# Expert attention with heads in 32-row tiles of TensorE, unpadded keys, and maxima taken over causal query blocks two units ahead

## The reference, cut to what matters

```
sx = einsum('bsh,ndh->bnsd', x, hl_w) + hl_b          # x is 32 x 188 x 64 after a layernorm
q = einsum('bnsd,neod->bneso', sx, wq)                # 4 heads n, 4 experts e, d = 16
k = einsum('bnsd,nod->bnso', sx, wk);  v = einsum('bnsd,nod->bnso', sx, wv)
scores = einsum('bnesd,bntd->bnest', q, k) * d**0.5 + causal
att = softmax(scores);  qkv = einsum('bnest,bntd->bnesd', att, v)   # 0 where sx == 0
gs = softmax(gate logits over experts); mixed = sum over e of qkv * gs
# then two layernorms over d, a small gated feed-forward, and the sum with x
```

## Time and profile before

| what | value |
|---|---|
| median of 3 runs | 1999.27 us (1997.89 to 2005.81) |
| profiled execution, its own time | 2006.71 us |
| its span in the trace | 2004.9 us |
| busy in the span: PE, PEld, DVE | 1719.6, 1344.4, 1488.5 us |
| busy in the span: ACT, POOL | 756.6, 690.5 us |
| mean granted TensorE clock | 0.865 |
| first and last record of `ex_R` | 572.9 and 1327.9 us |

### The profile page before, as it was taken

How to read it: one execution, slowest core, us unless ns; L and a number is a source line. 1 busy time by engine, 2 the same in 40 slices (tenths; PEclk the granted TensorE clock), 3 DMA queues, 4 the chain that set the end, 5 groups by cost and what they waited for, 6 DMA issues and landing times. The chain is left out here.

```text
span 2004.9 us, 45616 instructions
## 1 busy us (share of the span) xinstructions
PE 1719.6 (86%) x15064; PEld 1344.4 (67%) x15064; DVE 1488.5 (74%) x4423; ACT 756.6 (38%) x2274; POOL 690.5 (34%) x957
## 2 busy tenths in 40 slices
PE   1499999999769999999999999973999999788887
PEld 1266666666557777777777777752888888677776
DVE  6166676666627898888889888875766665688887
ACT  2245454545324444344344444321222222343442
POOL 2622222222134555545545445532211111322221
PEclk9999999999869999999999999985555555788788
DMA  2000000000000000000000000000000000000000
GB/s 114 1 2 0 0 0 0 0 0 0 1 1 1 1 2 0 0 0 0 0 0 0 0 0 0 1 1 0 1 0 0 0 0 1 1 5 8 4 6 11
DMA packets 6980, 8.13 MB, mean 4 GB/s; under 512 B 6272, under 2 KB 6272, under 8 KB 6784
## 3 DMA queue, kind: packets, MB, share of 16 engines
q1 hardware_dynamic: 6912, 7.25, 1.1%
HBM read 5.71 MB, written 1.54 MB: 4 GB/s over the span
## 5 line engine op out<-in xcount | busy, mean ns | idle before, releaser
L1142 ACT ACTIVATE ex_pT<-ex_T 128x376 f32<-128x376 f32 (+1 forms) x384 | 162.8, 440 | 217.1 <-PE ex_T L1044 207.9
L604 ACT ACTIVATE al_prob<-al_S,al_negmax 94x94 f32<-94x94 f32 (+1 forms) x512 | 146.2, 375 | 180.0 <-DVE al_negmax L731 180.0
L1207 DVE TENSOR_REDUCE ex_negmax<-ex_R 94x2 bf16<-94x376 f32 (+1 forms) x384 | 186.8, 543 | 30.6 <-PE ex_R L1015 30.0
L1044 PE MATMUL ex_T<-ex_qm,ex_kpad 128*128 128x188 f32 x1024 | 189.7, 329 | 0.0
L505 PE MATMUL al_S<-al_kpad,al_qT 128*94 128x376 f32 x384 | 166.5, 516 | 0.0
L1044 PEld LDWEIGHTS ex_T<-ex_qm,ex_kpad 128*128 128x128 f32 x1024 | 163.0, 192 | 5.1
L944 POOL TENSOR_SCALAR_AFFINE_SELECT ex_pT<-ex_pT 128x512 f32<-128x512 f32 x128 | 84.3, 659 | 236.5 <-ACT ex_pT L1142 236.5
L682 POOL TENSOR_TENSOR al_kpad<-al_kT,al_quad_mask 128x1504 f32<-128x1504 f32 x32 | 86.2, 2692 | 186.3 <-ACTq L619 186.3
L731 DVE TENSOR_REDUCE al_negmax<-al_S 94x2 f32<-94x376 f32 (+1 forms) x192 | 99.1, 542 | 62.6 <-PE al_S L506 56.7
L1554 POOL TENSOR_TENSOR ta_kk<-ta_ext 94x320 f32<-94x320 f32 x64 | 60.4, 961 | 246.4 <-DVE ta_qkn L1734 163.0
L1027 PE MATMUL ex_R<-ex_sxT,wsb 128*128 128x188 f32 x256 | 72.3, 364 | 47.5 <-DVE ex_negmax L1207 47.5
(11 more groups left out here) (308 smaller groups left out, 4300.8 us busy)
## 6 DMA issues: line engine op xcount, KB each, us to landing
tok_xin<-x_t SPq DMA_DIRECT2D x4, 760.0 KB, 6.9
wsb<-weights SPq DMA_DIRECT2D x1, 2531.0 KB, 14.2
out<-stream SPq DMA_DIRECT2D x16, 94.0 KB
tok_par<-tok_w SPq DMA_DIRECT2D x1, 4.5 KB, 1.7
```

The costliest lines, as they stand in the source:

```text
L604: last = nc.scalar.activation(p[:, k, cols], S[0:P, k, cols], ACT.Exp, bias=negmax[g % 2][:, m:m + 1])
L1044: last = nc.tensor.matmul(T[:, k, (j % 2) * N:(j % 2 + 1) * N], kpad[par][:, j, 0:K0], qm[e % 2][:], start=True, stop=True)
L1142: nc.scalar.activation(pT[e % 2][rows, k, cols], T[rows, k, cols], ACT.Exp)\
L1207: red(dst, src, AX.X, ALU.max, negate=True).then_inc(sem["r_used"], 1)
```

## The change: what it does

- **Heads in row tiles.** A head's 32 rows of keys and queries are used directly, as a 32-row tile of the array (`tile_position=(32 * n, ...)`). `kpad`, `kpadb`, `quad_mask` and GpSimd's two products a row are gone; ScalarE writes the keys twice instead, in fp32 and bf16.
- **Maxima over three causal blocks.** Queries are split in blocks of 64, 64 and 60, which meet 64, 128 and 188 keys. Two heads lie on the two halves of the partitions, two pairs in two banks of `R`: 12 matmuls of 32 rows x 64 columns, then 4 mask matmuls of 128 rows. VectorE's three reductions read 128, 256 and 376 elements.
- **queries** now writes to the free end of a bank of `T`, with six small matmuls instead of two.
- **scores** is split in heads 0 and 1 and heads 2 and 3, each head in its own bank of `T`; keys 64 to 191 (zero from 188 on) replace keys 128 to 187 in the second product. ScalarE's three exponents become two of 496 elements.
- **Order.** `max_scores` runs two units ahead, at the end of a unit before `weigh`. The order is: scores of heads 0 and 1, queries of the next unit, a fill, scores of heads 2 and 3, a fill, `max_scores`, `weigh`, a fill. The fills q01 and fc1 change places. VectorE's order is unchanged.
- More constants are set up by GpSimd ahead of the stage (29 instructions, from 21).

```diff
+    BLOCKS = [(0, QB, QB), (QB, 2 * QB, QB), (3 * QB, N, K1)]      # first column, keys, queries
+    PAIR = N + K1                                                  # QB = 64, QCOL = 256
-        kpad = two("kpad", [128, NH, N])
-        kpadb = two("kpadb", [128, NH, N], BF16)
+        kT = two("kT", [128, NP])
+        kTb = two("kTb", [128, N], BF16)
-        R = psum("R", [128, 3, 512])
-        T = psum("T", [128, 3, 512])
+        R = psum("R", [128, 2, 512])
+        T = psum("T", [128, NH, 512])
...
+                need(pe, sem["r_used"], 3 * u)
+                for k, (first, keys, _) in enumerate(BLOCKS):
+                    for n in range(NH):
+                        rows, side = slice(32 * n, 32 * n + 32), QB * (n % 2)
+                        nc.tensor.matmul(R[side:side + QB, n // 2, first:first + keys],
+                                         qTb[par][rows, e, QB * k:QB * (k + 1)], kTb[par][rows, 0:keys],
+                                         start=(k == 0), stop=False, tile_position=(32 * n, side), skip_group_check=True)
+                for b in range(2):
+                    two_blocks = R[:, b, 0:4 * QB].rearrange("p (a c) -> p a c", c=2 * QB)[:, :, 0:QB]
+                    nc.tensor.matmul(two_blocks, eye[:], block_mask[:].unsqueeze(1).broadcast_to([128, 2, QB]),
+                                     start=False, stop=True, skip_group_check=True)
+                    last = nc.tensor.matmul(R[:, b, 5 * QB:5 * QB + K1], eye[:], block_mask[:, 0:K1], start=False,
+                                            stop=True, skip_group_check=True)
+                last.then_inc(sem["r_full"], 1)
...
+                nc.tensor.matmul(T[:, 0, QCOL:QCOL + N], w("ewq")[:, e * 128:(e + 1) * 128], sxT[par][:, 0:N],
+                                 start=True, stop=False, skip_group_check=True)
+                for k, (_, _, cols) in enumerate(BLOCKS):
+                    for c in range(2):
+                        last = nc.tensor.matmul(T[:, 0, QCOL + QB * k:QCOL + QB * k + cols],
+                                                negmax[e % 2][:, k, 32 - 32 * c:160 - 32 * c], eye[:, QB * c:QB * c + cols],
+                                                start=False, stop=True, skip_group_check=True)
...
+                for s in range(2):
+                    for n in heads:
+                        rows = slice(32 * n, 32 * n + 32)
+                        if s == 0:
+                            last = nc.tensor.matmul(T[:, n, 0:N], kT[par][rows, 0:K0], qm[e % 2][rows, :], start=True,
+                                                    stop=True, tile_position=(32 * n, 0), skip_group_check=True)
                         else:
+                            last = nc.tensor.matmul(T[:, n, N:PAIR], kT[par][rows, QB:NP], qm[e % 2][rows, K0:N],
+                                                    start=True, stop=True, tile_position=(32 * n, 0),
+                                                    skip_group_check=True)
...
                     nr, ne, npar = (ru, e + 1, par) if e < 3 else (rf, 0, odd)
+                    fr, fe, fpar = (ru, e + 2, par) if e < 2 else (rf, e - 2, odd)
+                    last = None
+                    if valid(ru):
+                        last = scores(ru, par, e, (0, 1))
                     if valid(nr):
-                        max_scores(nr, npar, ne)
-                    if valid(ru):
-                        scores(ru, par, e)
+                        last = queries(nr, npar, ne)
+                    if last is not None:
+                        last.then_inc(sem["tA_full"], 1)
...
-                    if valid(nr):
-                        queries(nr, npar, ne)
+                    if valid(ru):
+                        scores(ru, par, e, (2, 3)).then_inc(sem["tB_full"], 1)
...
+                    if valid(fr):
+                        max_scores(fr, fpar, fe)
                     if e == 0 and valid(rt):
                         weigh(rt, odd, 3)
...
-                for k in range(3):
-                    dve.wait_ge(sem["r_full"], 3 * u + k + 1)
+                dve.wait_ge(sem["r_full"], u + 1)
+                for k, (first, keys, _) in enumerate(BLOCKS):
+                    red(negmax[e % 2][:, k, 48:113:64], R[:, :, first:first + keys], AX.X, ALU.max, negate=True)\
+                        .then_inc(sem["r_used"], 1)
```

More of the change, by code:

```diff
@@ L870, in expert_attention @@
         LN, FRONT, UNIT, TAIL, NORM, MLP, FIN, LAST = range(8)
[L873 to L876, removed]
+        FILLS = [("xT", FRONT), ("znT", MLP), ("sx", FRONT), ("k", FRONT), ("q01", FRONT), ("pickA", TAIL),
+                 ("fg", LAST), ("fc1", MLP), ("pickB", TAIL), ("q23", FRONT), ("v", FRONT), ("fc2", MLP)]
+        PER_ROW = {"sx": 2, "v": 2, "k": 2}
         def valid2(r):
@@ L940, in body @@
                         p = pT[e % 2]
-                        pool.wait_ge(sem["t_used"], 3 * (r * NE + e) + 3)
+                        pool.wait_ge(sem["tB_used"], r * NE + e + 1)
                         pool.sem_inc(sem["settled"], 1)
[L943 to L957, removed]
+                        for first, cols, shift in ((0, K0, 0), (N, K1, QB)):
+                            view = p[:, :, first:first + cols]
+                            nc.gpsimd.affine_select(out=view, in_=view, compare_op=ALU.is_ge, fill=0.0, base=shift,
+                                                    pattern=[[0, NH], [1, cols]], channel_multiplier=-1)\
+                                .then_inc(sem["causal_done"], 1)
                     r = t - LN
@@ L1036, in scores @@
+                return last
+            def scores(r, par, e, heads):
                 u = r * NE + e
                 if e == 0:
[L1038 removed]
+                    pe.wait_ge(sem["k_used"], 2 * (r + 1))
                 pe.wait_ge(sem["m_used"], u + 1)
[L1040 to L1045, removed]
[L1046 to L1049 removed]
+                if heads[0] == 0:
+                    pe.wait_ge(sem["tA_used"], u + 1)
+                else:
+                    need(pe, sem["tB_used"], u)
+                for s in range(2):
[4 more added lines that the diff above has]
+                                                    stop=True, tile_position=(32 * n, 0), skip_group_check=True)
+                        else:
+                            last = nc.tensor.matmul(T[:, n, N:PAIR], kT[par][rows, QB:NP], qm[e % 2][rows, K0:N],
+                                                    start=True, stop=True, tile_position=(32 * n, 0),
+                                                    skip_group_check=True)
+                return last
@@ L1123, in used @@
             def used(name, dst, rows, cols, func=ACT.Copy, **kw):
-                nc.scalar.activation(dst, X[rows, cols], func, **kw).then_inc(sem[name], 1)
+                src = X[rows, cols]
+                if len(dst.shape) == 3:
+                    src = src.rearrange("p (a n) -> p a n", a=dst.shape[1])
+                nc.scalar.activation(dst, src, func, **kw).then_inc(sem[name], 1)
             def body(t, par):
```

143 lines of the change are left out of this document (66 added, 77 removed).

## The result

The changed kernel takes 2393.09 us (median of 4 runs, 2390.87 to 2398.34) against 1999.99 us (1997.89 to 2005.81) for the kernel before beside it: a ratio of 1.196, 95% interval 1.193 to 1.200. It is slower by a fifth. The forecast was 2470 us, range 2070 to 2640. The profiled execution took 2394.03 us, with a span of 2392.3 us and a mean granted clock of 0.654 (before: span 2004.9, clock 0.865). The experiments' times are medians of all runs; ratios and differences leave out the runs that lie more than 1.5% above the fastest run of the same kernel.

What follows compares the result with a forecast made beforehand. TensorE was taken to set the pace at full clock, VectorE close behind. At half clock 14.8 us more a turn gave +474 over 32 turns, constants +3; from 2006.7 that made 2484, then 2476, forecast 2470 us, range 2070 to 2640.

Steps and rivals of the forecast that it cites:

- case A: Changed stage: TensorE's clock stays at half throughout; 2470 us, own range 2350 to 2600, chance 0.62.
- Case C: Changed stage: full clock throughout, waits as worked out, a turn of 26.5 us; about 2075 us, chance 0.08.
- The sum at half clock: Changed stage at half clock: TensorE's 35.4 us plus 3.6 of waits, a turn of 39.0 us against 24.2.
- a pair of S: Scores of two heads in row tiles at half clock: W's 1.14 us plus 0.1 for longer weight loads, 1.25.
- W: The `weigh` matmuls of one unit at half clock, unchanged: 1.14 us.
- M: The `max_scores` matmuls of one unit at half clock: 0.63 us, shape changes 0.3, loads 0.2, together 1.1.
- Q: The `queries` matmuls of one unit at half clock, with four more small ones and a change of shape: 1.4 us.
- fills and returns, a turn: TensorE's fills at half clock, 10.0 us a turn, and 0.2 a unit for return from row tiles.
- waits, a turn: TensorE's idle time at half clock, behind pickB 2.1, pickA 1.05, sx 0, turn's end 0.5: 3.6 us.
- a change of shape and its exposed load (0.3): Term in Q's price at half clock for changing tile shape and an exposed weight load: 0.3 us.
- Rival E: Row tiles don't run abreast, at half clock: +10 us a turn, about 2800 us, chance 0.06.
- Hidden, at nothing: ScalarE's two 496-element exponents, its second key copy and GpSimd's work cost nothing, or some tenths a turn without other TensorE waits.

Runs made afterwards that it cites:

- e3: Changed kernel with scores from padded fp32 keys on all 128 rows again, maxima still in row tiles: 2237.44 us, ratio 1.116 to the kernel before.
- e4: Changed kernel with the next unit's queries moved behind the second pair of scores, row tiles kept: 2253.49 us, ratio 1.126 to the kernel before.
- e8: e4's order with scores from padded fp32 keys on all 128 rows, nothing unused: 1977.99 us, ratio 0.989 to the kernel before.
- e2: Changed kernel with one burst of 64 unused 128-row bf16 matmuls in turn 7 only: 2398.57 us (one run).
- e1: Changed kernel with 12 unused 128-row bf16 matmuls ahead of each unit's queries: 2128.17 us, ratio 1.066 to the kernel before.
- e9: e8 with only heads 0 and 1 on padded keys, heads 2 and 3 in 32-row tiles: 2181.25 us.
- e10: e8 with only heads 2 and 3 on padded keys, heads 0 and 1 in 32-row tiles: 2009.63 us, ratio 1.005 to the kernel before.

## Why the prediction was right, and where it was off

**The clock, case A: right.** "I expect it never to rise" held to the last turn. The ground given, narrow work with waits, is what e3, e4 and e8 bear out: full-row scores alone give a clock of 0.82, e4's order alone 0.56, both 1.00. The prediction also gave entry at half clock as a ground. e2 shows that this was not needed: the clock was brought back once and was lost 17 us later; and the other kernels rose from the same entry. "So a fall is repaired only by dense full-array work" was put too strongly: in e4 the clock came back for short stretches among row tiles. The 395 us of the next stage, on which that sentence leans, are weaker evidence than they read: the matmuls there use 64 to 120 of the 128 rows, so they say little of tiles of 32 rows. That the tiles would lose the clock was a good guess before e4, not yet a reading.

**Case C and its rule: wrong here.** The Trainium skill (TensorE: Matmul & The Clock Gate, "What's actually happening") says that activity releases the throttle. In e4 TensorE was busy 97% of 720 us at a mean clock of 0.56; there the measurement decides, and being active was not enough. Of case C's waits e2 shows two at full clock, ahead of Q: 0.27 us behind sx and 1.24 behind pickA, against 0.55 and 1.5.

**The sum at half clock: right in kind, high by 2.45 us a turn**, 39.0 against 36.55.

| term, us | predicted | measured |
|---|---|---|
| a pair of S | 1.25 | 1.24 |
| W | 1.14 | 1.14 |
| M | 1.1 | 0.88 |
| Q | 1.4 | 1.13 to 1.24 |
| fills and returns, a turn | 10.8 | about 11.3 |
| TensorE busy, a turn | 35.4 | 33.96 |
| waits, a turn | 3.6 | about 2.6 |

The fills' measured value is what is left of 33.96 after 8 x 1.24 + 4 x (1.14 + 0.88) + 4.6 for Q. The mis-sized step is "a change of shape and its exposed load (0.3)", in Q and again in M: of Q's 1.13 us its first two records take 0.79 (1011.79 to 1012.58), the six small ones 0.34, and nothing is left for the 0.3. Q and M together are 1.9 us a turn below their terms, the fills 0.5 above. The second mis-sized term is the waits, 1.0 us too high: 0.69 behind pickA for 1.05 and 1.77 behind pickB for 2.1, named as said; the one behind sx came out at zero, as it was put, and at the turn's end 0.5 was foreseen and some 0.1 came. Over 32 turns 12.35 x 32 = 395 us, against 387.4 in the spans; 474 was forecast. The turns account for 79 us, the whole error of 77.

Three small slips in the sum change nothing of weight. 376 elements at half clock are 2.69 / 8 = 0.34 us by the row that it quotes, not 0.31, which makes M 1.2; 1.5 less the longer cover is 0.95, not 1.05; and the "two small fill records" in Q's price are Q's own two products with `negmax`.

**The smaller claims.** The maxima 1.08 us against 1.05; L1285 0.17, just under the "0.2 to 0.6"; constants +3.8 against +3; VectorE's relief was real and worth nothing while TensorE ran at half clock. It did not need the padded product gone altogether: e8 makes one a row again, and its counterpart of L1271 still takes 0.17 us; the product, shown below it, falls beside other work of VectorE:

```profile
1018.63 0.17 DVE L1294 TENSOR_SCALAR ex_zvar<-ex_zvar 94x16 f32<-94x16 f32 x1
```

```profile
1020.82 1.47 POOL L966 TENSOR_TENSOR ex_kpad<-ex_kT,ex_quad_mask 128x768 f32<-128x768 f32 x1
```

**Rival E, tiles not abreast: fell.** A pair of S costs what W does plus 0.1. The Trainium skill (TensorEngine Tiling (Array Packing), Gotcha 1: PSUM Pressure) says that row tiles can't use one PSUM bank at once. M, whose heads 0 and 1 share a bank on other partitions, took 0.88 us where 1.1 was allowed without that cost. Its twelve row-tiled records take 0.46 us (1007.61 to 1008.07), 380 elements for each head; two heads one after the other would take about 0.65 us, an estimate from the bf16 matmuls of the earlier trace rows, 1880 elements in 577.25 to 578.85. So the trace does not show that cost for two tiles in one bank on different partitions.

**Hidden, at nothing: wrong at full clock.** The prediction costed ScalarE at nothing, or some tenths a turn. At half clock no fill waits for it. At full clock three do in e1's turn, 0.65, 0.65 and 0.34 us, and in e2's 13 us of the kernel's own work two do, 0.28 and 0.66, the second 8 us behind the last unused matmul. ScalarE's timeline of e1 shows why:

```profile
1000.80 0.58 ACT L1161 ACTIVATE ex_pT<-ex_T 128x496 f32<-128x496 f32 x1 [1.86 <-PE ex_T L1031]
1001.28 0.32 ACT L1167 ACTIVATE ex_qm<-ex_T 128x188 f32<-128x188 f32 x1
1001.72 0.42 ACT L1144 ACTIVATE ex_kTb<-ex_X,ex_one_row 128x188 bf16<-128x188 f32 x1
1002.04 0.41 ACT L1144 ACTIVATE ex_kT<-ex_X,ex_one_row 128x188 f32<-128x188 f32 x1
```

The exponent of heads 0 and 1 waited 1.86 us and was released by Q's last record (L1031), since one semaphore speaks for those scores and for Q. Behind it, in order, come the masked queries and the copies of the fill, and the next fill needs their bank. Whatever holds Q back thus delays ScalarE's work, which does not need Q: in e1's row the 12 unused matmuls, in e2's row also the maxima, for which Q had itself waited 0.27 us. e4's order frees the exponent of heads 0 and 1; that of heads 2 and 3 now shares its semaphore with Q instead, and in e4's stage one fill waits for ScalarE, 0.2 us.

**What stays open.** The changed kernel's own order at full clock without unused work was seen for 13 us only (e2), so case C's 26.5 us a turn was not measured (27.2 with unused work, part of which fills waits). The runs tell that width, waits and place all weigh with the clock, not by what measure: where e9's and e10's falls stand is seen in the traces, but why the clock goes down behind e9's single wait of 1.07 us, and not behind e8's of 0.70, is not shown, since no run varies that wait alone.

## What to carry to other kernels

Packing small matmuls into tiles can make each of them faster and the kernel slower: before it, look at whether the stage holds its full clock with a margin (this one had already lost it for 3.4 us at 632.7), and price the plan at half clock too, from rows of the same trace that ran at it. Remove waits first (all that e8 gained), and narrow the matmuls second, one at a time, with the granted clock read after each; here the better order left narrow tiles 12.6% slower than before, and with wide scores it gained 1.1%. Where an in-order engine waits for one semaphore that speaks for two results, the later result's lateness is paid by everybody behind the earlier.

## What the runs showed of the hardware

- A TensorE busy 97% of a stage of row tiles ran at a mean granted clock of 0.56 (e4), and busy 33.91 of 34 us at 0.50; one as busy with scores on 128 rows ran at 1.00 (e8, 675.8 of 700 us).
- 64 wide bf16 matmuls in 9.87 us brought the clock from 0.50 to 1.00, and the same work as before lost it 17 us after it had come (e2).
- Two fp32 row tiles abreast: 0.69 us for a pair of heads at full clock and 1.24 at half, against 1.15 in the mean for the padded pair on all rows at full (e8).
- A VectorE operation on 16 elements a partition took 3.22 us beside GpSimd's padded product and 0.17 us without it. In e8 a reciprocal beside such a product took 0.25 us, as it did before.
